# Third cross attention: key weights folded two stages earlier, query work moved between its last gathers, decay table of layer 2 made in the stage before

## What is computed

```python
def _L1_attn_ref(xq, ...):                       # l1a
    xx = jnp.pad(x, ((0, 0), (1, 0), (0, 0)))[:, :-1]
    xr = x * time_mix_r + xx * (1 - time_mix_r)  # the same for k, v, g
    decay = jnp.exp(-jnp.exp(time_decay))
    pw = decay[:, None, None] ** jnp.maximum(diff - 1, 0)
    w_mat = jnp.where(diff > 0, pw, 0.0) + jnp.eye(T, dtype=x.dtype) * u[:, None, None]
    att = jnp.einsum('bhik,bhjk->bhij', rr, kk) * w_mat
    out = att @ vv
    ...
    return y * g @ W_o.T

def _L2_xattn_ref(q, k, v, ln_g, ln_b, w_in, ...):   # l2x, 8 heads of 128
    def proj(t):
        x = layer_norm(t, ln_g, ln_b) @ w_in.T
    f_q, f_k, f_v = (proj(q), proj(k), proj(v))
    cosine_sim = dots / (qn[..., :, None] * kn[..., None, :])
    k_ratio = 2.0 * jnp.minimum(k_var, 1.0) / (k_var + 1.0)
    var_component = jnp.einsum('hqn,hqm->hqnm', q_ratio, k_ratio)
    feat_corr = jnp.einsum('hnd,hne->hde', q_flat, q_flat) / q_flat.shape[1]
    cov_component = cosine_sim * decorr_scale
    weights = jax.nn.softmax(h1 @ wp_w2.T + wp_b2, axis=-1)   # h1 from the means of f_q, f_k
    mixed = cw * cosine_sim + vw * cov_component + ww * var_component
    out = jnp.einsum('hqnm,hqmd->hqnd', mixed, f_v)
```

## Time and profile before

| | us |
|---|---|
| median of 3 timed runs | 2849.14 (2844.96 to 2853.46) |
| profiled execution | 2843.44 |
| its span, first to last instruction | 2841.2 |
| of it: l1_attn (1508.9 to 1565.2) | 56 |
| l1_ffn (to 1645.3) | 80 |
| l2_xattn, to the first key projection (1680.3) | 35 |
| l2_xattn, key loop (to 2172.8) | 492 |
| l2_xattn, behind the loop (to 2216.6) | 44 |

### The profile page before, as it was taken

How to read it: one execution, slowest core, us unless ns; L and a number is a source line. 1 busy time by engine, 2 the same in 40 slices (tenths; PEclk the granted TensorE clock), 3 DMA queues, 4 the chain that set the end, 5 groups by cost and what they waited for, 6 DMA issues and landing times. The chain is left out here.

```text
span 2841.2 us, 59206 instructions
## 1 busy us (share of the span) xinstructions
PE 2372.3 (83%) x22114; PEld 1473.6 (52%) x22114; DVE 1839.3 (65%) x3061; ACT 1230.6 (43%) x1989; POOL 490.4 (17%) x282
## 2 busy tenths in 40 slices
PE   3399997999996576999994778999997458999978
PEld 3344433666664463666663734665555334555547
DVE  7566666888886516666643148777775667777721
ACT  2145554333332444777773213333331335555542
POOL 0045552000000000000000015555663000000000
PEclk6699998999998796999996889999998678999989
DMA  7467785566662265767650613222221136767626
GB/s 235 163 230 245 251 271 177 150 172 178 174 180 83 78 223 143 172 153 169 156 119 25 223 58 109 105 102 90 90 90 39 55 91 146 160 153 161 149 59 238
DMA packets 255634, 416.39 MB, mean 147 GB/s; under 512 B 32177, under 2 KB 216854, under 8 KB 255354
## 3 DMA queue, kind: packets, MB, share of 16 engines
q1 hardware_dynamic: 255482, 414.17, 50.7%
HBM read 323.26 MB, written 90.85 MB: 146 GB/s over the span
## 5 line engine op out<-in xcount | busy, mean ns | idle before, releaser
L2284 PE MATMUL l2x_kf<-l2x_w,l2x_nin 128*128 128x512 f32 x784 | 342.6, 597 | 6.7 <-DMA l2x_nin<-scratch_nT 6.6
L1479 DVE CUSTOM_DVE_ANT_0 l1x_junk<-l1x_pm,l1x_mrow,l1x_top 128x896 bf16<-128x896 f32 x224 | 247.1, 1148 | 117.0 <-PE l1x_pm L1633 105.7
L1479 DVE CUSTOM_DVE_ANT_0 l3x_junk<-l3x_pm,l3x_mrow,l3x_top 128x896 bf16<-128x896 f32 x224 | 246.0, 1148 | 88.8 <-PE l3x_pm L1633 88.3
L1561 ACT ACTIVATE l1x_prob<-l1x_ring,l1x_mask_col 128x512 f32<-128x512 f32 x392 | 247.8, 684 | 114.8 <-PE l1x_ring L1653 113.6
L1564 ACT ACTIVATE l3x_prob<-l3x_ring 128x512 f32<-128x512 f32 x392 | 213.0, 595 | 161.6 <-PE l3x_ring L1657 161.6
L2284 PEld LDWEIGHTS l2x_kf<-l2x_w,l2x_nin 128*128 128x128 f32 x784 | 148.9, 191 | 192.1 <-issue 189.6
L2266 ACT ACTIVATE l2x_fsq<-l2x_f 128x1024 f32<-128x1024 f32 x98 | 103.6, 1057 | 288.2 <-DVE l2x_f L2231 288.2
L1050 ACT ACTIVATE l0x_att_pt<-l0x_att_pt 128x1024 f32<-128x1024 f32 x99 | 104.7, 1058 | 261.7 <-DVE l0x_att_pt L989 261.7
L2330 POOL TENSOR_TENSOR l2x_gk<-l2x_f,l2x_ks 128x1024 f32<-128x1024 f32 x98 | 182.3, 1896 | 160.3 <-DVEq L2256 160.3
L1094 PE MATMUL l0x_att_pv<-l0x_wv,l0x_att_vin 128*128 128x512 f32 x392 | 194.4, 618 | 1.3 <-DVE l0x_att_tops L977 1.3
L2231 DVE TENSOR_TENSOR l2x_f<-l2x_kf,l2x_bias 128x1024 f32<-128x1024 f32 x98 | 120.0, 1225 | 88.2 <-PE l2x_kf L2284 76.3
(11 more groups left out here) (689 smaller groups left out, 4699.1 us busy)
## 6 DMA issues: line engine op xcount, KB each, us to landing
l1x_kt<-scratch_KS SPq DMA_DIRECT2D x84, 448.0 KB, 9.2
l3x_kt<-scratch_KS SPq DMA_DIRECT2D x84, 448.0 KB, 9.0
scratch_KT<-l0x_max_kf SPq DMA_DIRECT2D x28, 896.0 KB, 6.8
l0x_att_kt<-scratch_KT SPq DMA_DIRECT2D x56, 448.0 KB, 7.6
scratch_KS<-l0x_side_kp SPq DMA_DIRECT2D x14, 1344.0 KB, 13.7
scratch_KS<-l2x_side_kp SPq DMA_DIRECT2D x14, 1344.0 KB, 6.0
l0f_w<-L_ffn_exp_w SPq DMA_DIRECT2D x16, 1024.0 KB, 6.3
l1f_w<-L_ffn_W SPq DMA_DIRECT2D x16, 1024.0 KB, 6.2
```

Of the source, the lines that this page charges most:

```text
L1479: dve.tensor_tensor_reduce(junk[x % 2][:, :, :], pm[x % 2][:, :, 0:SPLIT], mrow[b][:, :].rearrange("p (s k) -> p s k", s=2), 1.0, top[1 - ...
L1561: ins = act.activation(into, scores, ACT.Exp, bias=R.mask_col[:, bass.ds(m * TILES + n // 4, 1)])
L2284: last = pe.matmul(pf[u][:, n, :], nin[b][:, c, t * P:(t + 1) * P], w[:, c, n * BANK:(n + 1) * BANK], start=(c == 0), stop=(c == DC - 1))
```

## The change

Two objects are made when l1_xattn begins and live on: `DecayWeights` (R.early) holds all tiles of l1_attn that don't depend on tokens, `FoldedKeys` (R.folded) the weights, bias row and first key chunk of l2_xattn.

- In l1_xattn SP issues four loads for the decay table ahead of the mask's way back (`load_decays`), and 15 more loads behind the first top rows (`last_sync`: 12 for l1_attn, 3 for l2_xattn). ScalarE makes the powers behind `ones_rows`, GpSimd the rate, the mask, the diagonal and 1 - mix.
- In l1_attn the loads and the table are gone. The scales go to ScalarE, the multiply-adds stay on VectorE, each pair joined by a semaphore; TensorE waits for two halves at a time.
- In l1_ffn TensorE makes l2_xattn's bias row behind the router, ScalarE copies it out, GpSimd folds the gain, and SP loads the first key chunk behind the last expert weights.
- l2_xattn has two blocks in the place of four. It begins with the key loop. SP's order changes: each key chunk's load goes one spill earlier. The norms and all query work down to the correlation are behind the loop on VectorE and ScalarE, and inside the last gather on TensorE (`query`, before tiles 0, 3 and 6). M is copied out in the same block. Small loads of the gating network go out first.

```diff
                     top_to_rows(0, 0)
+                    lead.last_sync(sp)
 
...
                     q.gpsimd(pool)
+                    lead.gpsimd(pool)
...
     n_tiles = R.keys // P
+    R.folded = FoldedKeys(nc, A)
...
                 heads.load_stack(sp, 0, 0)
+                R.early.load_decays(sp)
                 sp.wait_ge(S.sem("mask_out"), 16)
                 heads.load_mask(sp, 0, 0)
...
                 heads.ones_rows(act)
+                R.early.powers(act)
+
+            def gpsimd(self, pool):
+                R.early.gpsimd(pool, R.ident)
+
+            def last_sync(self, sp):
+                R.early.load_weights(sp)
+                R.folded.load(sp)
 
             def vector(self, dve):
...
+            nin = [folded.first, sb("nin1", [P, DC, CHUNK])]
+            nw, nw2 = sb("nw", [P, 16]), sb("nw2", [P, 16])
...
+            xn, xn2, xT = [nin[1][:, 0, n * DIM:(n + 1) * DIM] for n in range(3)]
+            qc, corr = [t[:, :].rearrange("p (h d) -> p h d", h=H) for t in sq]
...
-                    with sp.Fori(0, steps) as i:
-                        for b in range(2):
-                            after(sp, S.counted(f"nin_used{b}"), i)
-                            sp.dma_start(nin[b][:, :, :], src[bass.ds(i * 2 + b, 1)].squeeze(0)).then_inc(
-                                S.counted(f"nin{b}"), 16)
-                            side.load(sp, 2 * i + b)
-                            side.spill(sp, i, b)
+                    def load(i, b):
+                        sp.dma_start(nin[b][:, :, :], src[bass.ds(i * 2 + b, 1)].squeeze(0)).then_inc(
+                            S.counted(f"nin{b}"), 16)
+
+                    def even(i):
+                        after(sp, S.counted("nin_used1"), i)
+                        sp.sem_inc(S.sem("load_begun"), 1)
+                        load(i, 1)
+                        side.load(sp, 2 * i)
+                        side.spill(sp, i, 0)
+
+                    def odd(i):
+                        side.load(sp, 2 * i + 1)
+                        side.spill(sp, i, 1)
+
+                    small(sp.dma_start(wp1[:, :, :], by_rows(A["L2_xattn_wp_w1"])))
+                    small(sp.dma_start(b1[:, :], A["L2_xattn_wp_b1"].partition_broadcast(H)))
+                    small(sp.dma_start(lg[:, :], A["L2_xattn_wp_ln_g"].partition_broadcast(H)))
+                    small(sp.dma_start(lb[:, :], A["L2_xattn_wp_ln_b"].partition_broadcast(H)))
+                    small(sp.dma_start(w2[:, :], A["L2_xattn_wp_w2"]))
+                    small(sp.dma_start(b2[:, :], A["L2_xattn_wp_b2"].partition_broadcast(H)))
+                    with sp.Fori(0, steps - 1) as i:
+                        even(i)
+                        after(sp, S.counted("nin_used0"), i + 1)
+                        sp.sem_inc(S.sem("load_begun"), 1)
+                        load(i + 1, 0)
+                        odd(i)
+                    even(steps - 1)
+                    odd(steps - 1)
                     side.finish(sp, steps)
...
+                    link = Link(dve, S.sem("q_link"))
+                    link(dve.memset(ones[:, :], 1.0))
+                    link(dve.tensor_scalar(off[:, :], R.ident[:, :], -1.0, 1.0, ALU.mult, ALU.add))
+                    norm_vector(dve, link, S, "n", R.x[:, :], xn, nw)
+                    norm_vector(dve, link, S, "m", xn, xn2, nw2)
+                    turn_vector(dve, S, "m", xT.rearrange("p (c t) -> p c t", c=DC), pt)
+                    dve.wait_ge(S.sem("q_proj"), 1)
+                    fqh = fq[:, :].rearrange("p (h d) -> p h d", h=H)
+                    link(dve.tensor_tensor(fq[:, :], pf[0][:, :, :].rearrange("p a n -> p (a n)"), bias[:, :], ALU.add))
+                    link(dve.tensor_reduce(qs[:, 0, :], fqh, AX.X, ALU.add))
+                    link(dve.tensor_scalar(cs[:, :], qs[:, 0, :], 1.0 / HD, None, ALU.mult))
+                    dve.tensor_tensor(qc, fqh, cs[:, :].unsqueeze(2).broadcast_to([P, H, HD]), ALU.subtract).then_inc(
+                        S.sem("qc"), 1)
+                    link(dve.tensor_tensor(corr, fqh, fqh, ALU.mult))
+                    dve.tensor_reduce(qs[:, 1, :], corr, AX.X, ALU.add).then_inc(S.sem("qss"), 1)
+                    dve.wait_ge(S.sem("qss"), 1)
+                    head_stats(dve, link, None, qs[:, 0, :], qs[:, 1, :], None, qs[:, 3, :], qs[:, 4, :], H)
+                    dve.wait_ge(S.sem("qn"), 1)
+                    link(dve.reciprocal(qs[:, 2, :], qs[:, 2, :]))
+                    dve.wait_ge(S.sem("corr"), 1)
+                    link(dve.tensor_tensor(corr, heads(pf[1][:, :, :]), off[:, :].unsqueeze(1).broadcast_to([P, H, P]),
+                                           ALU.mult))
+                    link(dve.tensor_tensor(corr, corr, corr, ALU.mult))
+                    dve.tensor_reduce(cs[:, :], corr, AX.X, ALU.add).then_inc(S.sem("corr_sq"), 1)
+                    dve.wait_ge(S.sem("q_mean"), 1)
+                    dve.tensor_scalar(gT[:, 0, :], pc[:, 0:H], 1.0 / P, None, ALU.mult).then_inc(S.sem("gT"), 1)
+                    after(dve, S.counted("f_used1"), steps)
...
                     def project(i, b):
-                        after(pe, S.counted(f"nin{b}"), (i + 1) * 16)
+                        if b == 0 and isinstance(i, int) and i == 0:
+                            pe.wait_ge(folded.S.sem("first"), 16)
+                        else:
+                            after(pe, S.counted(f"nin{b}"), (i + b) * 16)
...
-                    def gather(i, b):
+                    def query(step):
+                        if step == 0:
+                            turn_tensor(pe, S, "m", xn2, pt, R.ident)
+                            pe.wait_ge(S.sem("m_xT"), 1)
+                            for n in range(2):
+                                for c in range(DC):
+                                    last = pe.matmul(pf[0][:, n, :], xT[:, c * P:(c + 1) * P],
+                                                     w[:, c, n * BANK:(n + 1) * BANK], start=(c == 0),
+                                                     stop=(c == DC - 1))
+                            last.then_inc(S.sem("q_proj"), 1)
+                        if step == 3:
+                            pe.wait_ge(S.sem("qc"), 1)
+                            for h in range(H):
+                                last = pe.matmul(pf[1][:, h // 4, (h % 4) * P:(h % 4 + 1) * P], qc[:, h, :],
+                                                 qc[:, h, :], start=True, stop=True)
+                            last.then_inc(S.sem("corr"), 1)
+                            for h in range(H):
+                                last = pe.matmul(pc[:, h:h + 1], fq[:, h * HD:(h + 1) * HD], ones[:, 0:1],
+                                                 start=True, stop=True)
+                            last.then_inc(S.sem("q_mean"), 1)
+                        if step == 6:
+                            pe.wait_ge(S.sem("corr_sq"), 1)
+                            pe.matmul(pt[:, 0:H], ones[:, :], cs[:, :], start=True, stop=True).then_inc(
+                                S.sem("corr_total"), 1)
+
+                    def gather(i, b, beside=None):
                         after(pe, S.counted(f"ratio{b}"), i + 1)
                         for t in range(TILES):
+                            if beside:
+                                beside(t)
...
+                    folded.wait_all(pe)
...
-                    gather(steps - 1, 1)
+                    gather(steps - 1, 1, query)
...
+    def powers(self, act):
+        S = self.S
+        act.wait_ge(S.sem("decay_loads"), self.decay_loads.total)
+        act.activation(self.td[:, :], self.td[:, :], ACT.Exp).then_inc(S.sem("rates"), 1)
+        act.wait_ge(S.sem("rate"), 1)
+        for h in range(self.H):
+            last = act.activation(self.wm[:, h, :], self.lag[:, :], ACT.Exp, scale=self.td[:, h:h + 1])
+        last.then_inc(S.sem("powers"), 1)
+
+    def gpsimd(self, pool, ident):
+        S, H = self.S, self.H
+        link = Link(pool, S.sem("decay_link"))
+        pool.wait_ge(S.sem("rates"), 1)
+        pool.tensor_scalar(self.td[:, :], self.td[:, :], 1e30, -1.0, ALU.min, ALU.mult).then_inc(S.sem("rate"), 1)
+        link(pool.tensor_tensor(self.att[:, :, :], ident[:, :].unsqueeze(1).broadcast_to([P, H, P]),
+                                self.u[:, :].unsqueeze(2).broadcast_to([P, H, P]), ALU.mult))
+        pool.wait_ge(S.sem("powers"), 1)
+        link(pool.tensor_tensor(self.wm[:, :, :], self.wm[:, :, :],
+                                self.later[:, :].unsqueeze(1).broadcast_to([P, H, P]), ALU.mult))
+        pool.tensor_tensor(self.wm[:, :, :], self.wm[:, :, :], self.att[:, :, :], ALU.add).then_inc(
+            S.sem("decays"), 1)
+        pool.wait_ge(S.sem("loads"), self.loads.total)
+        pool.tensor_scalar(self.omm[:, :, :], self.mixc[:, :, :], -1.0, 1.0, ALU.mult, ALU.add).then_inc(
+            S.sem("omm"), 1)
...
+                dve.wait_ge(S.sem("xp"), 1)
```

(43 more changed lines are left out.)

270 lines of the change are left out of this document (100 added, 170 removed).

## The result

The changed kernel takes 2801.29 us (median of 4 runs, 2794.54 to 2803.38) where the kernel before takes 2847.75: ratio 0.9836, 95% interval 0.9815 to 0.9857. Five more runs gave 2796.39 against 2845.98, ratio 0.9822 (0.9808 to 0.9835). So it is 46 to 50 us faster; forecast were 51.6 and 2797.5. Both kernels' stages can be laid side by side, since none overlaps the next. The two columns on the right are two profiled executions of the same changed kernel, in us.

The account below looks back on a forecast made before the run. TensorE bounds the key loop; elsewhere chains of small steps make it wait. Terms +1.0 - 21.4 + 0.5 - 28.9 - 4.6 + 1.8 = -51.6 us took the 2849.1 median to 2797.5, range 2785 to 2812.

Parts of the forecast that it names:

- Layer 2 attention, -21.4: l1_attn: early loads and table, scales on ScalarE, projections after two pairs; 21.4 us gained, ends 18.6 and 23.4.
- l1_xattn, +1.0: Layer 2 cross attention: table work hidden, four loads ahead of the first mask row cost between 0 and 1.8 us, taken +1.0.
- Rival 3: l1_xattn: early weight loads hold chunk 1's keys or chunk 2's mask row, up to 7.3 us, 2804.8; chance 0.03.
- Layer 2 feed-forward, +0.5: l1_ffn: eight bias passes delay the expert choice's spread, later passes run at full clock; between +2.6 and -1, taken +0.5.
- GpSimd's fold beside the expert products: l1_ffn: GpSimd's fold of the key weights was to lie beside the expert products; no separate cost given.
- the lock: VectorE and GpSimd take one SBUF port pair in turns, each for a whole instruction; 1.2 us counted in the tail.
- Opening, -28.9: l2_xattn's start: clearing matmuls at 1647.5 instead of 1676.41, first chunk on chip; 28.9 us gained, ends 27 and 31.5.
- Turn, -4.6: l2_xattn, chunk 0 to 1: earlier load saves 8.5 us, waiting for VectorE costs 3.9; 4.6 gained, between 0 and 8.5.
- Loop, 0: l2_xattn's other 12 chunks: loads come earlier but TensorE is the bound, so the 34 us period stays.
- Tail, +1.8: l2_xattn, last gathers to gating network: query work moves into the last chunk, costing 1.8 us; ends -2.5 and +8.
- Rival 1: Clock up: full clock for clearing matmuls, output products and part of query projection, 6.5 us more gain, 2791.0; chance 0.10.
- Rival 2: Tail: six small norm operations each wait half a GpSimd product, 5.6 us more, 2803.1; chance 0.12.

Follow-up runs that it names:

- The fillers: Changed kernel plus idle TensorE multiplications, results unread, between last gather and output products: 66 gave ratio 0.9861 to the kernel before, 31 gave 0.9828.
- the norms first: Changed kernel with the query's norms, ones and mask made by VectorE ahead of its key loop in l2_xattn: ratio 0.9817 to the kernel before.

## Why the prediction was right, step by step

The two large terms came out for the reasons given, and the sum was right with them. What it missed, taken together, is 0.7 and 6.0 us in the two traces, the gain smaller than forecast in both.

*Layer 2 attention, -21.4.* Measured -21.5 and -21.2, by the steps named: the scores ended 12.9 us behind the transposition, 13.0 by my sum.

*l1_xattn, +1.0.* Measured -0.1 and -0.8. VectorE's first maximum came 24.6 and 23.4 us behind the transposition, 24.3 before, so the four loads ahead of the mask row cost 0.3 us at most. GpSimd's table work ended at 1094.8, ScalarE still idled 12 us before its next operation, and the 15 loads took 7.4 us of SyncE without anyone waiting. Rival 3 falls.

*Layer 2 feed-forward, +0.5.* Measured +2.7 and +1.9, at my upper end of +2.6; the other seven traces with the same l1_ffn have +1.3 to +3.2. The spread went as said (2.1 late, 1.7 back). A step that failed is "GpSimd's fold beside the expert products": it starts with the bias's end, 6 us ahead of them, and met VectorE's copies, 0.9 us, shown by holding it back. I had looked for the lock only in the tail. I also took the clock as up for good; but it fell in VectorE's next 3.8 us, and the product took 5.5 and 7.0 us to the first relu, no better than the 5.6 of before; where TensorE had worked through, it took 3.96.

*Opening, -28.9.* Measured -29.8 and -30.1. The start of the clearing matmuls moved by 28.8 us; the rest is TensorE's clock, which let them take 2.5 and 3.3 us instead of 3.8, while the first projection took 25.4 and 24.2 instead of 24.9. *Turn, -4.6.* Measured -2.5 and -4.3. The wait for VectorE was 3.4 us, 3.9 by my sum; mis-sized was the restart behind it, which I had at full clock: 19.13 us for 40 passes in one execution, 17.43 in another. Of the eleven traces with the new order, nine have 18.9 to 20.5 behind the same wait and two 17.43, so the turn is mostly worth 1 to 3 us. Why the same wait costs nothing in some executions stays open.

*Loop, 0.* 417.6 us in all three traces.

*Tail, +1.8.* Measured +1.5, the idling for the norms 5.3 us, the mask 1.3 longer by the lock, the projection 5.52 where I had 6.2. The interleaving is worth 4.9 us.

*Output stage.* The step that the sum lacked: I had ended it at the gating network's first matmul, because the code behind is unchanged. It takes 1.8 to 2.4 us more, 4.1 in the first trace. TensorE's clock stays at half in the transpositions and in part or all of the products. The fillers show that cause for all but 0.4 us; why the clock rose in time before and in the kernels with a shifted tail (3.72 us in each), and not here, stays open.

Rival 1 (the clock up, -6.5) came true in small part: some 2 us in the clearing matmuls, layer 2 attention's output products (6.95 and 6.61 us instead of 7.01) and the query projection. In l1_ffn, the turn and the output stage the clock went the other way. Rival 2 didn't happen: of the norms' operations beside GpSimd only the scalings grew, from 0.41 to 0.57 and 0.59 us. Its mechanism is real, though, and hit once the order was changed: two small operations took 1.82 us each. Here the rule that I had cited, the Trainium skill, SBUF — State Buffer, "SBUF: two separate sides", is borne out by three runs: copies, the mask and two-input operations of VectorE waited until GpSimd's instruction had ended, while the key loop's bias addition, from PSUM, kept 1224 ns in the mean beside them. Over all, the stages came out 6.0 and 0.7 us above the sum of -51.6 in the two traces: the misses in l1_ffn, the turn and the output stage (up to +2.2, +2.1, +4.1), less up to 3 us by which l1_xattn and the opening did better.

## What to carry to other kernels

Where a chain of small steps is shortened, read which engine will stand still next and for how long: a pause costs its own length and then, at times, the clock behind it (5.3 us of waiting and 2 us of clock in the tail here, 3.4 and 0 to 3 in the turn). Filling a wait pays when the work fits into it, at the clock that holds there: with eight passes in one wait the first relu of l1_ffn came 1 to 3 us later than without them (0.9 of it by the lock), with four in each and the fold held back almost 3 us earlier. A sum must not end where the edited code ends, but where the times of old and new run in parallel again.

## What the runs showed of the hardware

The same 16 output products took 3.72 us at a granted clock of 0.94 to 1.00 and 6.77 at 0.50, and values between (5.2 to 5.8) in five executions whose code is the same there. The 40 passes behind the same wait of 3.4 us took 17.4 us in two executions and 18.9 to 20.5 in nine.

GpSimd's product of 1024 columns and some of VectorE's operations on SBUF held each other up in both directions: 1.22 us became 2.9, and 13.1 us for seven products became 15.0; even operations on 8 columns took 1.82 us instead of 0.17. Not held up beside the same products were VectorE's sums over one input (1.22 us), the norms' statistics (0.43) and operations on one column (0.15). The squares that took 2.91 us with the norms first took 1.22 in the changed kernel, where they began 3.6 us behind GpSimd's end: what an operation costs depends on where the order puts it.
